# Six slots from one search on masked slots, and the shared experts of two token chunks run where the six parts are added

## The reference, cut to what matters

```python
logits = jnp.einsum('th,eh->te', x, gate_w)
scores = jax.nn.softmax(logits, axis=-1)
topk_w, topk_ids = jax.lax.top_k(scores, TOP_K)            # TOP_K = 6 of 64
topk_w = topk_w / (jnp.sum(topk_w, axis=-1, keepdims=True) + EPS)
comb = comb.at[jnp.arange(T)[:, None], topk_ids].add(topk_w)
act = jax.nn.silu(g) * u * comb[:, :, None]                # g, u: each expert's gate and up products
routed = jnp.einsum('tef,ehf->th', act, w_down)
shared = jnp.einsum('tf,hf->th', jax.nn.silu(sg) * su, ws_down)
return routed + shared
```

## Time and profile before

| | |
|---|---|
| profiled execution, its own time | 1435.55 us |
| its span | 1433.8 us |
| median of 3 runs | 1438.24 us |
| PE / DVE / ACT / POOL busy | 1258.0 / 792.2 / 431.5 / 506.3 us |
| mean granted clock of PE | 0.934 |
| route / experts / combine | 840 to 955 / 955 to 1387 / 1387 to 1434 us |

### The profile page before, as it was taken

The page is one execution under the profiler, slowest core; times in us unless marked ns, Lnnn a source line. Parts: engine busy times, 40 slices in busy tenths (PEclk is TensorE's granted clock), DMA queues, the critical chain, the costliest instruction groups (busy, mean ns, idle before and its releaser), DMA issues. The chain is left out here.

```text
span 1433.8 us, 21660 instructions
## 1 busy us (share of the span) xinstructions
PE 1258.0 (88%) x6348; PEld 885.3 (62%) x6348; DVE 792.2 (55%) x2106; ACT 431.5 (30%) x843; POOL 506.3 (35%) x606
## 2 busy tenths in 40 slices
PE   5789988988899999967999979749999999999940
PEld 3455555656788888844555556436777777777730
DVE  6568777724534343364545447984555555555546
ACT  2225544555423232222334421101222222222200
POOL 6013342333100000021200000966777777777720
PEclk9969999999999999989899989868999999999975
DMA  7888755401000000038443012027666666643329
GB/s 278 235 184 128 104 86 83 75 4 49 8 0 1 1 1 1 1 111 285 117 114 102 19 33 64 3 71 240 187 196 196 196 179 195 206 142 84 55 89 322
DMA packets 106751, 159.25 MB, mean 111 GB/s; under 512 B 24135, under 2 KB 56891, under 8 KB 106656
## 3 DMA queue, kind: packets, MB, share of 16 engines
q1 hardware_dynamic: 78720, 110.64, 29.8%
q0 software_dynamic: 15264, 34.78, 9.1%
q10 hardware_dynamic: 12672, 12.58, 2.7%
HBM read 117.55 MB, written 48.30 MB: 116 GB/s over the span
## 5 line engine op out<-in xcount | busy, mean ns | idle before, releaser
L1801 PE MATMUL experts_ps_gu<-experts_wgu,experts_xt 128*128 x636 | 228.4, 482 | 3.0 <-SPq L1762 1.6
L921 DVE TENSOR_REDUCE att_mx<-att_ps 128x1 f32<-128x512 f32 (+3 forms) x240 | 151.8, 652 | 90.3 <-PE att_ps L721 53.4
L721 PE MATMUL att_ps<-stacks_ks,stacks_qs 96*128 96x512 f32 (+4 forms) x384 | 157.2, 477 | 29.5 <-PEq L165 16.1
L1931 POOL DMA_INDIRECT y_parts<-experts_y,moe_target x159 | 161.7, 1017 | 59.5 <-issue 36.9
L1925 POOL DMA_INDIRECT experts_x<-x_rows,moe_source x159 | 157.2, 989 | 58.6 <-issue 45.5
L1848 ACT ACTIVATE experts_xt<-experts_ps_x 128x256 f32<-128x256 f32 x159 | 61.1, 384 | 346.5 <-PE experts_ps_x L1790 344.5
L1821 PE MATMUL experts_ps_y<-experts_wd,experts_ht 96*128 x636 | 163.9, 380 | 0.0
L857 ACT ACTIVATE att_pt<-att_ps 128x1024 f32<-128x1024 f32 (+3 forms) x160 | 121.8, 764 | 134.6 <-PE att_ps L743 134.0
L1801 PEld LDWEIGHTS experts_ps_gu<-experts_wgu,experts_xt 128*128 128x128 f32 x636 | 109.3, 191 | 69.9 <-issue 36.8
L1879 DVE COPY experts_ht<-experts_ps_h 96x256 f32<-96x256 f32 x159 | 66.9, 421 | 131.2 <-PE experts_ps_h L1811 131.2
L721 PEld LDWEIGHTS att_ps<-stacks_ks,stacks_qs 96*128 96x128 f32 (+1 forms) x384 | 80.2, 214 | 81.6 <-issue 43.5
(11 more groups left out here) (217 smaller groups left out, 2249.1 us busy)
## 6 DMA issues: line engine op xcount, KB each, us to landing
experts_wgu<-L_ffn_w_gate_up SPq DMA_DIRECT2D x64, 352.0 KB
stacks_qs<-q_parts SPq DMA_DIRECT2D x112, 128.0 KB, 3.5
stacks_ks<-k_parts SPq DMA_DIRECT2D x112, 128.0 KB, 5.2
combine_got<-y_parts ACTq DMA_DIRECT2D x24, 512.0 KB, 9.6
experts_wd<-L_ffn_w_down SPq DMA_DIRECT2D x64, 176.0 KB
v<-stacks_values SPq DMA_DIRECT2D x4, 1024.0 KB, 6.5
stacks_vs<-v SPq DMA_DIRECT2D x16, 256.0 KB, 6.1
dense_words<-codes SPq DMA_DIRECT2D x3, 1024.0 KB, 10.3
```

The lines of the kernel that those rows point to most:

```text
L721: ins = pe.matmul(out, qs[a][z][0:rows_a, h, i * P:(i + 1) * P], ks[a][z][0:rows_a, h, 0:width(i)], start=a == 0, stop=a == last_part and ...
L921: dve.tensor_reduce(mx[:, hs[0]:hs[-1] + 1, i], ps_1[:, (u.n * ng + g) % 2, 0:len(hs) * width(i)] .rearrange("p (h w) -> p h w", h=len(hs) ...
L1801: ins = pe.matmul(ps_gu[:, u.bank, 0:2 * FE], xt[:, u.bank, k, :], at_place(wgu, u, k), start=k == 0, stop=k == KD - 1)
L1931: pool.indirect_dma_start(out=parts_dram[:, :], out_offset=bass.IndirectOffsetOnAxis(ap=target[:, n:n + 1], axis=0), in_=y[n % L][:, :], i ...
```

## The change

It does the following.

- In route the softmax isn't divided out. `max` finds the eight largest exponentials; the last two of the list are overwritten, `match_replace` marks the six in place, and a comparison makes the mask. The sums and weights go to a row of 64 weights per token (zero where not chosen), written by POOL; a gathered row then has 320 numbers instead of 272.
- The counts come to one expert per partition; PE makes the running sums over experts by triangular matrices and adds the experts' starts to the counts in PSUM (`add_starts`). The count of an expert is taken as at least one.
- Slots that a token hasn't chosen are multiplied by zero; a `max` of eight on each token's row gives all six slots at once. Any order of the six serves.
- Tile marks: POOL does k = 0, 2, 4; ACT does 1, 3, 5 as Relu(1 - Abs(number - tile)). DVE marks cells.
- Tile owners are spread by a matmul with the identity instead of two DMAs.
- Only chunks 0 and 1 of the shared experts are computed in route. DVE adds them to x inside the last tiles of the expert loop (after tiles 155 and 157). Chunks 2 and 3 are computed in `add_parts`, on PE, ACT and DVE, beside the adding of the parts. The loads of the parts move to SP's queue, the stores to ACT's.
- The down weights are padded on the host (192 KB instead of 176 KB a load), so their memset goes, and the wait of the weight loads for it. The counter of finished tiles starts at 0 instead of 1, and its waits count one less.

The diff, cut to its core:

```diff
...
+ROW = D + NE
...
+EARLY = 2
+SHAPED = 9
...
+            pool.wait_ge(weights_done, 1)
+            pool.tensor_tensor(rows[:, :, D:ROW], chosen[:, :, :], row2[:, :, :].to_broadcast(full), ALU.mult)\
+                .then_inc(rows_set, 1)
+            pool.wait_ge(split_done, 1)
             for k in range(TOP):
                 if on_pool(k):
...
+            def mark_tiles(k, h):
+                n = k // 2 * 2 + h
+                if n == 0:
+                    act.wait_ge(split_done, 2)
+                wait(act, tiles_set, n - 1)
+                for i in range(half):
+                    ins = act.activation(distance[h][:, i, :], iota_a[:, :], ACT.Abs,
+                                         bias=tile_neg[:, h * half + i, k:k + 1])
+                ins.then_inc(distances_set, 1)
+                act.wait_ge(distances_set, n + 1)
+                act.activation(at_tile[:, k, h * half:(h + 1) * half, :], distance[h][:, :, :], ACT.Relu,
+                               bias=one[:, :], scale=-1.0).then_inc(tiles_set, 1)
...
+            act.wait_ge(shaped, SHAPED)
+            gate(1, 0)
+            take(0)
+            gate(1, 1)
+            mark_tiles(1, 0)
+            gate(1, 2)
+            mark_tiles(1, 1)
+            take(1)
+            for k in (3, 5):
+                for h in range(2):
+                    mark_tiles(k, h)
...
+            def count():
+                pe.wait_ge(shaped, SHAPED)
+                pe.wait_ge(mask_done, 1)
+                for j in range(NTT):
+                    ins = pe.matmul(ps_count, mask_bf[:, j, :], ones[:, :], start=j == 0, stop=j == NTT - 1)
+                ins.then_inc(counted, 1)
...
+                for b in range(2):
+                    pe.matmul(slots[:, b * half:(b + 1) * half, :], before[:, :], mask_bf[:, b * half:(b + 1) * half, :],
+                              start=True, stop=False)
+                    for j in range((b + 1) * half - 1):
+                        i = max(j + 1, b * half)
+                        n = (b + 1) * half - i
+                        pe.matmul(slots[:, i:i + n, :], ones[:, :],
+                                  mask_bf[:, j, :].unsqueeze(1).to_broadcast([P, n, NE]), start=False, stop=False)
+            def add_starts():
+                pe.wait_ge(tiles_known, 1)
+                pe.matmul(ps_until, tiles[:, :], tiles_until[:, :], start=True, stop=True)
+                for b in range(2):
+                    ins = pe.matmul(slots[:, b * half:(b + 1) * half, :], tiles[:, :],
+                                    tiles_before[:, :].unsqueeze(1).to_broadcast([NE, half, NE]), start=False, stop=True)
                 ins.then_inc(placed, 1)
+            def turn_owner():
+                pe.wait_ge(owned, 1)
+                for j in range(2):
+                    n = (NTILE + 1 - j) // 2
+                    ins = pe.matmul(ps_owner[:, j::2], tile_owner[:, j, :], ident_bf[:, 0:n], start=True, stop=True)
+                ins.then_inc(owner_turned, 1)
...
+            count()
+            count_before()
+            add_starts()
             gate_up(1, 0)
+            pe.wait_ge(until_read, 1)
             down(0)
             gate_up(1, 1)
             gate_up(1, 2)
-            gate_up(2, 0)
-            count_before()
+            turn_owner()
             down(1)
...
             for k in range(TOP):
                 turn_back(k)
...
-            dve.tensor_reduce(row[:, :, :], exps[:, :, :], AX_X, ALU.add)
+            for i in range(NTT):
+                dve.max(top[:, i, :], exps[:, i, :])
+            mul(0, 0)
             dve.drain()
-            dve.reciprocal(row2[:, :, :], row[:, :, :])
+            dve.tensor_reduce(chosen_total[:, :, :], top[:, :, 0:TOP], AX_X, ALU.add)
             dve.drain()
-            dve.tensor_tensor(scores[:, :, :], exps[:, :, :], row2[:, :, :].to_broadcast(full), ALU.mult)
+            dve.memset(top[:, :, TOP:8], -2.0)
             dve.drain()
-            mul(0, 0)
-
             for i in range(NTT):
-                dve.max(top[:, i, :], scores[:, i, :])
+                dve.match_replace(left[:, i, :], top[:, i, :], exps[:, i, :], -1.0)
             dve.drain()
+            dve.tensor_scalar(mask_bf[:, :, :], left[:, :, :], 0.0, None, ALU.is_lt).then_inc(mask_done, 1)
             mul(0, 1)
-            for i in range(half):
-                dve.max_index(idx[:, i, :], top[:, i, :], scores[:, i, :])
             mul(0, 2)
...
+            dve.tensor_reduce(total[:, :, :], exps[:, :, :], AX_X, ALU.add)
+            dve.scalar_tensor_tensor(out=chosen[:, :, :], in0=left[:, :, :], scalar=0.0, in1=exps[:, :, :],
+                                     op0=ALU.is_lt, op1=ALU.mult)
             dve.drain()
-            dve.tensor_copy(idxf[:, :, :], idx[:, :, :])
-            dve.tensor_scalar(row2[:, :, :], row[:, :, :], TOP_EPS, None, ALU.add)
+            dve.scalar_tensor_tensor(out=row[:, :, :], in0=total[:, :, :], scalar=TOP_EPS, in1=chosen_total[:, :, :],
+                                     op0=ALU.mult, op1=ALU.add)
             dve.drain()
...
-
-            dve.tensor_scalar(count[:, :], ps_n, float(P - 1), None, ALU.add).then_inc(counted, 1)
+            dve.reciprocal(row2[:, :, :], row[:, :, :]).then_inc(weights_done, 1)
+            dve.wait_ge(counted, 1)
+            dve.tensor_scalar(count[:, :], ps_count, 1.0, float(P - 1), ALU.max, ALU.add)
             dve.drain()
             dve.tensor_scalar(tiles_i[:, :], count[:, :], P.bit_length() - 1, None, ALU.logical_shift_right)
             dve.drain()
-            dve.tensor_copy(tiles[:, :], tiles_i[:, :])
+            dve.tensor_copy(tiles[:, :], tiles_i[:, :]).then_inc(tiles_known, 1)
+            dve.wait_ge(placed, 1)
+            dve.tensor_copy(until[:, :], ps_until).then_inc(until_read, 1)
+            dve.scalar_tensor_tensor(out=slot[:, :, :], in0=slots, scalar=1.0, in1=mask_bf[:, :, :],
+                                     op0=ALU.add, op1=ALU.mult)
             dve.drain()
...
+            for i in range(NTT):
+                dve.max(top_slot[:, i, :], slot[:, i, :])
             dve.drain()
...
+            dve.tensor_scalar(slot_i[:, :, :], top_slot[:, :, :], -1.0, None, ALU.add)
+            dve.drain()
+            dve.tensor_scalar(tile_i[:, :, :], slot_i[:, :, :], P.bit_length() - 1, None, ALU.logical_shift_right)
+            dve.tensor_scalar(cell_i[:, :, :], slot_i[:, :, :], P - 1, None, ALU.bitwise_and)
+            dve.drain()
+            dve.tensor_copy(tile_f[:, :, :], tile_i[:, :, :]).then_inc(split_done, 1)
+            dve.tensor_scalar(tile_neg[:, :, :], tile_i[:, :, :], -1.0, None, ALU.mult).then_inc(split_done, 1)
+            dve.tensor_copy(cell_f[:, :, :], cell_i[:, :, :])
+            mul(1, 0)
+            dve.tensor_tensor(passed[:, :, :], until[:, :].unsqueeze(1).to_broadcast([P, 2, NE]),
                               iota_t[:, :].unsqueeze(2).to_broadcast([P, 2, NE]), ALU.is_le)
+            dve.tensor_copy(plan.end[:, :], until[:, :])
             dve.drain()
-            dve.tensor_scalar(start[:, :], incl[1 - z][:, :], float(P), None, ALU.mult)
-            dve.tensor_scalar(plan.end[:, :], last[:, :], 1.0, None, ALU.add)
             dve.tensor_reduce(first[:, :, :], passed[:, :, :], AX_X, ALU.add)
             dve.drain()
...
+            dve.tensor_scalar(tile_owner[:, :, :], first[:, :, :].to_broadcast([P, 2, P]), float(NE - 1), None,
+                              ALU.min).then_inc(owned, 1)
             mark_cells(0)
-            pick(1)
-            mul(2, 2)
+            mul(1, 1)
+            mul(1, 2)
             mark_cells(1)
-            mul(3, 0)
-            pick(2)
             mark_cells(2)
-            mul(3, 1)
-            pick(3)
+            dve.wait_ge(owner_turned, 1)
+            dve.tensor_copy(plan.owner[:, :], ps_owner)
+            dve.tensor_scalar(plan.order[:, :], ps_owner, 1.0, None, ALU.add)
             mark_cells(3)
-            mul(3, 2)
-            pick(4)
             mark_cells(4)
-            mark_tiles(2)
-            pick(5)
             mark_cells(5)
-            mark_tiles(5)
             for k in range(TOP):
...
-                sp.dma_start(wd[0:FEP, z, :, :], w2[e].rearrange("(p k) d -> p k d", k=2)).then_inc(weights_loaded[z], 16)
+                sp.dma_start(wd[:, z, :, :], w2[e].rearrange("(p k) d -> p k d", k=2)).then_inc(weights_loaded[z], 16)
...
-                dve.scalar_tensor_tensor(out=picked[:, :], in0=x[u.flight][:, ROW_ID:ROW_ID + TOP],
-                                         scalar=plan.owner[:, bass.ds(u.n, 1)], in1=x[u.flight][:, ROW_W:ROW_W + TOP],
+                dve.scalar_tensor_tensor(out=picked[:, :], in0=plan.numbers[:, :],
+                                         scalar=plan.owner[:, bass.ds(u.n, 1)], in1=x[u.flight][:, D:ROW],
                                          op0=ALU.is_equal, op1=ALU.mult, accum_out=share[u.flight][:, :])\
...
+            def add_shared(c):
```

(61 more changed lines are left out.)

264 lines of the change are left out of this document (86 added, 178 removed).

## The result

The changed kernel takes 1404.92 us (median of 4 runs, 1402.76 to 1406.05), the kernel before 1438.68 (4 runs, 1436.84 to 1441.55). The ratio is 0.9762, 95% interval 0.9742 to 0.9782: 33.8 us less. The profiled execution took 1402.76, its span is 1401.0 against 1433.8.

The account below looks back on a forecast made before the run. Routing was taken as bound by the chain of slots, marks, turning and folding, the experts by PE, combine by DMA. -36.2 - 1.1 + 1.2 + 6.9 = -29.2 gave 1406.4 profiled, 1408 as median, range 1399 to 1421.

Parts of the forecast that it names:

- Routing, -36.2: Routing block: slots of all six tables at 874.3, three mark chains ending near 909, block ending at 919.0; -32 to -39.
- the 37.0 that the prediction gives for that case: Routing: length of GpSimd's 48 marks at 0.77 if VectorE's mark_cells delays them too, 2.4 us more than the term.
- Start of the experts, -1.1: Start of expert block: without the padding memset weights are requested earlier, 1.1 us of TensorE's wait goes; 0 to -1.6.
- Loop, 0: Expert loop: larger weights and wider gathered rows stay hidden, and width costs GpSimd nothing; 0.
- Tail sums, +1.2: End of expert loop: the second of two VectorE sums stands before the last hidden tile's copy; +1.2, 0 to 2.4.
- Combine, +6.9: Combine block: VectorE, in order, waits for TensorE's products, last add at 50.0 instead of 43.1; +6.9, 2.8 to 31.
- the first: Rival, routing: Abs and Relu need their own table and Abs takes 0.40, ScalarE ends at 917; 1416 in all, chance 0.09.
- Combine's clock: Rival, combine: TensorE's clock stays at 0.50 throughout, +31 instead of +6.9; 1432, chance 0.05.
- The gather by width: Rival, expert loop: GpSimd's gather costs by width, 0.98 to 1.15, its turn 2.77; +16, 1424, chance 0.05.
- The search: Rival, routing: match_replace takes 1 us apiece, 13 us lost, 1421; slots no earlier than now, 1431; chance 0.06.

Follow-up runs that it names:

- e1: The changed kernel once more, same code: 1405.80 us, ratio 0.9779 to the kernel before.
- e10: The changed kernel once more, same code, beside e9: 1405.34 us, ratio 0.9768 to the kernel before.
- e7: Changed kernel with VectorE's memset of the down weights' padding back and the weight loads waiting for it: 1409.10 us, ratio 0.9786 to the kernel before.
- e12: The kernel of e7 once more, to see TensorE's clock: 1408.33 us in one run.
- e9: Changed kernel with e4 and e6 together and the loop's two sums after tiles 147 and 149: 1401.39 us, ratio 0.9750 to the kernel before.
- e4: Changed kernel with VectorE's products and shared sums placed behind later adds in combine, same work: 1401.58 us, ratio 0.9747 to the kernel before.
- e6: Changed kernel with two of six mark tables on GpSimd instead of three, VectorE making the fifth: 1402.43 us, ratio 0.9746 to the kernel before.
- e3: Changed kernel with three chunks of the shared experts in routing and one in combine: 1405.95 us, ratio 0.9782 to the kernel before.
- e2: Changed kernel with all four chunks of the shared experts kept in routing: 1414.49 us, ratio 0.9844 to the kernel before.

## Why the prediction came out as it did

The forecast for the profiled execution was 1406.4, measured 1402.76; the sum was -29.2 and the span fell by 32.8, of which 0.4 is that routing began earlier. By its steps:

- **Routing, -36.2: measured -34.8** (59.43 to 45.03, and the marks 20.44 earlier against the start of routing). The mechanism held: marks at 875.3 on the forecast's scale for 874.3, 48 marks in 34.86 for 34.6, GpSimd, ScalarE and VectorE ending at 909.75, 908.98 and 907.1, within 4 us as forecast, 10.2 to the first gather for 10.0. Of the 1.4 too much, 1.0 is that the marks began late, and one row explains that and more: route_tiles_i took 1.92, its neighbour of the same size 0.22. It starts 0.06 us after GpSimd's weighted row of 1.90 and ends with it. The prediction put that row there as covered work and asked only what it would cost GpSimd. 0.195 us for a replacement, 4.0 for half a table on ScalarE and 0.72 from mark to mark (34.86 / 48 = 0.73) were right. The marks of up to 2.06 us are gone: the longest now takes 0.83. A mark takes 0.77 beside VectorE's cell marks and 0.68 while VectorE waits, but neighbours overlap, so 48 of them didn't come to the 37.0 that the prediction gives for that case. Two of its figures are slips on which nothing hangs: the slope gives 1.24 for the Relu, not 1.3 (it took 1.35), and 24 wide matmuls, not 22, stream the 8704 columns.
- **Start of the experts, -1.1: measured -0.8** (first gather to first gate_up 8.32 to 7.55; 8.15 and 7.60 in e1 and e10).
- **Loop, 0: measured -3.4**, the step that the forecast had wrong. Tile time, DMA share (0.71) and GpSimd's turn are as forecast, but the step took the clock at the loop's start over from the kernel before, without a term. From the first gate_up to combine's first load it took 423.9 us and then 421.2, of which the tail's sums are 0.7, so 3.4 went; the fourth gate_up starts 9.1 us after the first (936.54 - 927.47), before 12.8. Whether the change made it is not shown: the changed kernel had the early clock 3 times of 3, the kernel before the late one 2 of 2, but the same kernel had both in e7 and e12.
- **Tail sums, +1.2: measured 0.7.** VectorE's timeline before the last hidden copy, and GpSimd beside it:

```profile
1338.34 1.22 DVE L1896 TENSOR_TENSOR all_x<-all_x,shared_out 128x1024 f32<-128x1024 f32 x1
1338.70 1.71 POOL L1917 DMA_INDIRECT y_parts<-experts_y,moe_target  x1 [1.34 <-DVE experts_y L1874]
1339.47 0.41 DVE L1865 COPY experts_ht<-experts_ps_h 96x256 f32<-96x256 f32 x1
```

  The sum does stand before that copy, which comes 1.1 us later against the last gate_up's start (1374.88 before, 1335.40 here), near the forecast. But GpSimd's last three puts run back to back, and hid a part of it: from the last gate_up to combine's first load it is 12.54 us in both profiles of the kernel before, 13.22 or 13.23 in all eleven with the sums there, and 12.49 in e9, with the sums eight tiles earlier. The put of 1.71 us instead of 0.98 delays the two behind it by 0.73, about as much; which of the two ended last is not separated.
- **Combine, +6.9: measured +6.0.** Product 5 ended 29.7 after the first load (forecast 29.8), the sum of chunk 2 at 32.0 (32.4), down(3) at 39.2 (41.0), the last add at 49.0 (50.0). The clock fell as it had in routing, but down(3) lost 1.75 us by it (7.11 - 5.36) and not 3.2. e4 shows that the mechanism was VectorE's order.
- **The rivals.** No table load before Abs or Relu, so the first is out; the trace agrees with the Trainium skill ("ScalarE: Activation LUTs", section "Table sets: the hidden batching unit"), by which relu and abs are in every table set. Combine's clock was back at 2.4 GHz by 1355.02, 6.4 us after its first load (1.88 for four matmuls that took 3.75). The gather by width is out by the row below. The search was as short as it says.

The groups by line, GpSimd's gather and put (busy us, mean ns | idle before):

```profile
L1917 POOL DMA_INDIRECT y_parts<-experts_y,moe_target x159 | 163.1, 1026 | 56.7 <-issue 37.5 <-DVE experts_y L1874 9.8 <-DVE experts_picked L1882 9.4
L1911 POOL DMA_INDIRECT experts_x<-x_rows,moe_source x159 | 155.1, 976 | 58.3 <-issue 47.4 <-DVE experts_picked L1882 7.6 <-PE experts_ps_x L1777 3.4
```

A gather of 1280 B takes 976 ns on average, 989 at 1088 B in the kernel before, a put of 1024 B 1026: width doesn't count here.

The median moved by 33.8, 1 more than the profiled spans, and the prediction's 1408 lay 3.1 above it. In the profile the clock at the loop's start is all but the whole miss, since the other misses (+1.4, +0.3, -0.5, -0.9) cancel, which is luck. Whether the three runs without a profile had the early clock too is not known: their mean granted clock is 0.945 to 0.947 for the profiled one's 0.952, but the profiles of e1 and e10 have the early clock at 0.947.

## What to carry to other kernels

When several engines make parts of one result, write the end of each chain down, and the engine's other work ahead of it: the gain of unloading one ends at the next (e6 took 11.9 us of marks off GpSimd and won 2.8; e3 won nothing). An engine that takes its work in order must not meet an operand that is still to be computed while work that is ready stands behind it; e4 won 4 us by order alone. Price the start of a stage at both levels of TensorE's clock, and compare by stages, since executions of one kernel differed by 6 us in all.

## What was not expected of the hardware

- **The clock after a pause.** TensorE starts the expert loop at 1.2 GHz; over 14 profiles 8 have one gate_up at that level and 6 have three, nothing between, and the stage is 428 to 429.4 or 431.8 to 434.2 us long. The granted clock rose 3.0 to 3.8 us after the first gate_up's start in the 8, 12.4 to 13.6 after it in the 6. No single cause tested (weights, tables) decides it.
- **VectorE and GpSimd hold each other up**, in both directions: the integer tensor_scalar of 1.92 beside a GpSimd tensor_tensor (0.22 for its neighbour), and GpSimd's put of 1.71 beside a VectorE sum of two SBUF operands (0.98 for the others near the loop's end). Every put that began 0.36 us after such a sum took 1.71 or 1.72, in eleven profiles; one of e2 that began 0.69 after it took 1.38; the two of e9 that began 0.37 and 0.18 before theirs took 1.02, as puts in the loop do. The Trainium skill ("SBUF — State Buffer", section "Who interferes with whom") says that the two engines share a pair of ports, that a tensor_scalar can enter a mode that takes it, and that whoever issues first keeps it for the whole instruction; the first row agrees. For the second it says that two SBUF inputs on VectorE hold up a GpSimd instruction that reads SBUF; the puts agree, by their order too, if a put's issue is one, which no run here shows.
